# An autocorrelation layer in a pipeline of 16 pairs: the top-8 mask taken from the raw correlation, the bias copied into PSUM

## The reference, cut to what matters

```python
x = layernorm(x + attn(x))          # a 4-layer network of width 64, a scan over time, projection back to 512
x = layernorm(x + xattn(x, ctx))    # autocorrelation attention, below
x = layernorm(x + ffn(x))           # both factors quantised to MXFP4 in blocks of 32, product 512x512, + bias
```

```python
corr = ifft(fft(q) * conj(fft(k))).real          # over the 64 times, per channel
w, idx = top_k(corr, 8)                           # the 8 largest lags of each channel
w = softmax(w)
out = sum_i w[i] * v[min(idx[i] + t, 63)]         # values taken at shifted times
```

## Time and profile before

| what | value |
|---|---|
| median of three runs | 321.19 us |
| the profiled execution | 323.65 us |
| its span, first to last instruction | 321.6 us |
| mean granted TensorE clock | 0.978 |
| PE busy | 274.6 us (85%) |
| DVE busy | 269.8 us (84%) |
| ACT busy | 231.1 us (72%) |
| POOL busy | 174.7 us (54%) |

### The profile page before, as it was taken

The page is one execution under the profiler, slowest core; times in us unless marked ns, Lnnn a source line. Parts: engine busy times, 40 slices in busy tenths (PEclk is TensorE's granted clock), DMA queues, the critical chain, the costliest instruction groups (busy, mean ns, idle before and its releaser), DMA issues.

```text
span 321.6 us, 4437 instructions
## 1 busy us (share of the span) xinstructions
PE 274.6 (85%) x1060; PEld 109.8 (34%) x1060; DVE 269.8 (84%) x871; ACT 231.1 (72%) x541; POOL 174.7 (54%) x226
## 2 busy tenths in 40 slices
PE   1597988989889887888998999999998888977762
PEld 1223222322222222254433554434444244422220
DVE  5969989889888894358999999999999989869580
ACT  6046789899799797967666687778877776745534
POOL 1026513204204014023378888999999999997842
PEclk9999899999999999999999999999999999979987
DMA  6999999602113200600000000111101102011122
GB/s 207 396 273 354 325 160 213 128 23 65 36 33 85 78 0 17 116 1 2 2 0 16 17 14 6 50 49 18 51 34 51 51 16 51 34 50 49 51 82 99
DMA packets 22576, 26.54 MB, mean 83 GB/s; under 512 B 10771, under 2 KB 11411, under 8 KB 22550
## 3 DMA queue, kind: packets, MB, share of 16 engines
q1 hardware_dynamic: 20470, 22.06, 21.9%
q0 software_dynamic: 2080, 4.19, 7.7%
HBM read 15.89 MB, written 4.19 MB: 62 GB/s over the span
## 4 chain that ended last, share of the span: by engine, by line
DVE 30%; ACT 20%; PE 18%; issue 15%; POOL 11%; DMA 3%; SPq 1%; POOLq 0%; DVEq 0%; ACTq 0%
DVE big L1172 5%; DVE m L1153 4%; DVE X L1107 3%; DVE big L1142 3%; DMA big<-in_xT_dram 3%; PE ps L380 3%; ACT big L654 3%; DVE ps L1203 3%; ACT L752 2%; DVE ps L1081 2%; ACT X L682 2%; PE ps L562 2%; POOL big L925 2%; POOL big L931 2%; DVE big L1277 2%
## 5 line engine op out<-in xcount | busy, mean ns | idle before, releaser
L654 ACT ACTIVATE big<-X,lnv 128x512 f32<-128x512 f32 x48 | 34.2, 713 | 15.0 <-DVE X L1107 15.0
L1107 DVE SCALAR_TENSOR_TENSOR X<-ps,X 128x512 f32<-128x512 f32 x48 | 32.1, 682 | 10.7 <-PE ps L415 6.1
L391 PE MATMUL ps<-ctx_ring,consts 64*128 64x512 f32 (+1 forms) x96 | 35.8, 643 | 0.0
L441 PEld LDWEIGHTS ps<-consts,big 96*128 96x128 f32 x256 | 29.8, 191 | 13.4 <-issue 10.6
L441 PE MATMUL ps<-consts,big 96*128 96x64 f32 x256 | 32.0, 278 | 1.1 <-DVE big L1142 1.1
L1184 DVE TENSOR_TENSOR big<-ps,ctxf 128x512 f32<-128x512 f32 x48 | 30.8, 683 | 2.0 <-PE ps L475 1.3
L682 ACT ACTIVATE X<-X,lnv 128x512 f32<-128x512 f32 x32 | 25.8, 808 | 0.6
L1172 DVE MATCH_REPLACE8 big<-w,big 128x64 f32<-128x64 f32 x128 | 25.1, 210 | 0.0
L838 POOL TENSOR_TENSOR big<-big 128x512 f32<-128x512 f32 x4 | 5.8, 1444 | 35.5 <-DVE big L1250 25.5
L918 POOL TENSOR_TENSOR big<-big 128x512 f32<-128x512 f32 x15 | 19.0, 1268 | 6.2 <-DVE big L1172 6.0
L1142 DVE TENSOR_TENSOR big<-ps,ctxf 96x512 f32<-96x512 f32 x32 | 20.4, 677 | 0.8 <-PE ps L428 0.8
(11 more groups left out here) (188 smaller groups left out, 675.9 us busy)
## 6 DMA issues: line engine op xcount, KB each, us to landing
big<-in_xT_dram SPq DMA_DIRECT2D x4, 1024.0 KB, 9.4
ctx_ring<-in_ctx_dram SPq DMA_DIRECT2D x16, 256.0 KB, 4.0
out_dram<-X SPq DMA_DIRECT2D x16, 256.0 KB, 2.0
X<-in_x_dram SPq DMA_DIRECT2D x2, 1536.0 KB, 11.4
X<-rows_sb POOLq DMA_DIRECT2D x1, 3072.0 KB, 21.6
X<-in_wq_dram SPq DMA_DIRECT2D x1, 1024.0 KB, 5.6
X<-in_x_dram SPq DMA_DIRECT2D x2, 512.0 KB, 3.9
X<-rows_sb POOLq DMA_DIRECT2D x1, 1024.0 KB, 8.0
```

Of the source, the lines that this page charges most:

```text
L391: mm(bank(LANE_BANK[lane]), mat((CY_0, CY_1, CY_C)[f])[half, :], ctx_ring[half, r * N:(r + 1) * N], start=True, stop=True).then_inc(s_cfor ...
L441: last = mm(ps[:, 2 * N + j * P + b * L:2 * N + j * P + (b + 1) * L], PQ[0:EVEN, b * N + j * P:b * N + (j + 1) * P], mat(IC_E)[0:EVEN, 0:L ...
L654: squared[k, n] = chain(a(JUNK[k], row(n), ACT.Square, bias=st[:, 0:1], scale=-float(V), accum_out=st[:, 2:3]))
L1107: stt(row(m), bank(b), 0.0, row(m), ALU.add, ALU.add, accum_out=st[:, 0:1]).then_inc(s_sum[k], 1)
```

## The change

The network of the first 125 us is left as it is. In the pipeline:

- **The mask.** match_replace now runs on the raw correlation: `largest_taken` (once `without_largest`) replaces the eight maxima in `CR` by -3e38 (`TAKEN`) and writes `REST`. It needs the maxima only, not the exponentials. The masked weight is then `WN = (REST == TAKEN) * G`, one scalar_tensor_tensor on DVE for every pair (`chosen`). POOL's subtraction (L918), POOL's shifted maxima (L908) and ACT's exponential of them (L711) are gone, with `w8`. `CR` of a pair is now kept until its `REST` is written.
- **The rounding constant.** On DVE L1203 and L1204 become one tensor_tensor, `exponents`: `VB` and a one-element column `field` (broadcast), bitwise and, into `MB` in SBUF. The clip and multiply that was L1204 is a tensor_scalar on POOL in `clamped`.
- **The bias.** It was split into three bf16 rows and added by a matmul (L520). Now it is broadcast to 128 partitions by a second transfer into `rows_sb`, and ACT copies it in fp32 from SBUF into bank 1 (`bias_in`) after `fed` of the pair before; the four matmuls add onto it. The splitting on DVE in the first microseconds (L1056 to L1067) and one small transfer go.
- **The order of every loop.** The order of calls and their depths are new on PE, ACT, POOL and DVE. The counts of `kept_busy` change, and it now stands behind `feed_forward`.

```diff
-DRAIN_BUSY = ((0, 4), (6, 6), (5, 3))
+DRAIN_BUSY = {LAST + 7: 10, LAST + 8: 12}
+TAKEN = -3.0e38
+EXPONENT = 0x7F800000
@@ sync
-            sp.dma_start(rows_sb[0:SPLIT, V:2 * V], rows[V:2 * V].partition_broadcast(SPLIT)).then_inc(s_brow, 16)
-            sp.dma_start(rows_sb[:, 0:V], rows[0:V].partition_broadcast(P)).then_inc(s_rows, 16)
+            for k in range(2):
+                sp.dma_start(rows_sb[:, k * V:(k + 1) * V], rows[k * V:(k + 1) * V].partition_broadcast(P)
+                             ).then_inc(s_rows, 16)
...
-            for n in range(PAIRS + 3):
+            for n in range(PAIRS + 5):
                 quantized_to_channels(n)
-                stored(n - 3)
+                stored(n - 5)
@@ tensor, feed_forward
-                    if n >= 1:
-                        pe.wait_ge(s_sum[2], n)
-                    pe.wait_ge(s_magic[1], min(n + 2, LAST))
-                    mm(bank(1), ones[:, :], bias3[:, :], start=True, stop=False)
+                    pe.wait_ge(s_bias, n + 1)
@@ tensor, loop
-            for t in range(1, PAIRS + 11):
-                weights_to_time(t - 7)
-                out_even(t - 8)
-                weight_rest_forms(t - 7)
-                weight_forms(t - 7)
-                correlation(t - 5)
...
-                query_forms(t - 4)
-                feed_forward(t - 10)
...
-                quantized_to_channels(t - 9)
...
-                out_rest(t - 7)
-                projection(t)
+            for t in range(1, PAIRS + 10):
+                out_even(t - 6)
+                if t == 2:
+                    mixed(SLOTS)
+                    transposes(0, VC, bank(7), XQ[0])
+                weight_rest_forms(t - 5)
+                weight_forms(t - 5)
...
+                projection(t)
+                correlation(t - 3)
                 quantized_to_channels(t - 9)
+                feed_forward(t - 9)
+                query_forms(t - 2)
+                if t in DRAIN_BUSY:
+                    pe.wait_ge(s_sum[0], PAIRS)
+                    kept_busy(DRAIN_BUSY[t])
+                out_rest(t - 5)
+                weights_to_time(t - 4)
@@ scalar
+            def bias_in(n):
+                if here(n):
+                    if n == 0:
+                        act.wait_ge(s_rows, 32)
+                        act.wait_ge(s_hn, 2)
+                    else:
+                        act.wait_ge(s_sum[2], n)
+                    copy(bank(1), rows_sb[:, V:2 * V]).then_inc(s_bias, 1)
...
-                        act.wait_ge(s_m8, n - 1)
+                        act.wait_ge(s_mr, n - 1)
...
-                    a(w8[:, :], w8[:, :], ACT.Exp).then_inc(s_g, 1)
                     a(G, G, ACT.Exp).then_inc(s_g, 1)
...
-            for t in range(PAIRS + 10):
...
+            for t in range(-1, PAIRS + 9):
+                squares(1, t - 5)
+                factors(1, t - 5)
+                normalise(1, t - 5)
+                probabilities(t - 3)
+                corr_out(t - 2)
+                factors(0, t)
+                squares(2, t - 9)
+                last_factors(t - 9)
+                weights_out(t - 3)
+                top_exponentials(t - 2)
+                normalise(0, t)
...
+                log_sum(t - 2)
+                bias_in(t - 7)
+                squares(0, t + 1)
...
+                quantized_out(t - 8)
@@ gpsimd
-                    chain(g_.tensor_tensor(groups(w8[:, :], TOP), top, sh.broadcast_to([P, NG, TOP]), ALU.subtract))
...
-                    g_.tensor_tensor(WN, G, REST, ALU.subtract).then_inc(s_wn, 1)
...
+            def clamped(n):
+                if here(n) and n < LAST:
+                    pool.wait_ge(s_expo, n + 1)
+                    chain(g_.tensor_scalar(MB, MB, 0.25, MAGIC, ALU.max, ALU.mult))
+                    chain.then_wait(g_.tensor_scalar(VB, VB, 1.5, -1.5, ALU.min, ALU.max))
+                    halfway[n] = chain(g_.tensor_tensor(VB, VB, MB, ALU.add))
...
-            for t in range(PAIRS + 8):
-                block_scaled(t - 3)
-                chosen(t - 1)
-                top_differences(t)
-                finished(t - 7)
-                mark = clamped(t - 3)
-                differences(t)
-                rounded_off(t - 3, mark)
+            for t in range(PAIRS + 9):
+                differences(t - 1)
+                clamped(t - 4)
+                rounded_off(t - 4)
+                top_differences(t)
+                block_scaled(t - 3)
+                finished(t - 9)
@@ vector
+            def largest_taken(n):
+                if here(n):
+                    dve.wait_ge(s_m8, n + 1)
                     if n >= 1:
                         dve.wait_ge(s_wn, n)
+                    top = m8[:, n % 2 * NG * TOP:(n % 2 + 1) * NG * TOP]
                     for g in range(NG):
+                        last = v_.match_replace(REST[:, g * L:(g + 1) * L], top[:, g * TOP:(g + 1) * TOP],
+                                                CR[n % 2][:, g * L:(g + 1) * L], TAKEN)
                     last.then_inc(s_mr, 1)
...
-                    do(ts(bank(1).bitcast(I32), VB.bitcast(I32), 0x7F800000, None, ALU.bitwise_and))
-                    ts(MB, bank(1), 0.25, MAGIC, ALU.max, ALU.mult).then_inc(s_magic[1], 1)
+                    tt(MB.bitcast(I32), VB.bitcast(I32), field[:, 0:1].broadcast_to([P, V]), ALU.bitwise_and
+                       ).then_inc(s_expo, 1)
+            def chosen(n):
+                if here(n):
+                    dve.wait_ge(s_g, n + 1)
                     dve.wait_ge(s_mr, n + 1)
+                    if n >= 1:
+                        dve.wait_ge(s_wt, n)
+                    stt(WN, REST, TAKEN, G, ALU.is_equal, ALU.mult).then_inc(s_wn, 1)
...
-            for t in range(PAIRS + 9):
-                attended(t)
-                weight_products(t - 6)
-                block_scales(t - 7)
-                without_largest(t - 5)
-                last_chosen(t - 5)
-                fed(t - 9)
-                last_quantized(t - 7)
-                largest(t - 4)
-                if t == 6:
-                    last_norm(1, RS_LAST)
-                rounding(t - 7)
-                top_sum(t - 4)
-                query_products(t - 3)
-                crossed(t - 6)
+            for t in range(PAIRS + 10):
+                query_products(t - 3)
+                top_sum(t - 4)
+                crossed(t - 6)
+                exponents(t - 7)
+                last_quantized(t - 7)
+                largest_taken(t - 4)
+                weight_products(t - 5)
+                block_scales(t - 6)
+                attended(t)
+                if t == 5:
+                    last_norm(1, RS_LAST)
+                chosen(t - 4)
+                largest(t - 3)
+                fed(t - 9)
```

107 lines of the change are left out of this document (24 added, 83 removed).

## The result

The changed kernel takes 333.76 us in the median (330.56 to 337.26), the kernel before 321.24 beside it: ratio 1.0332, 95% interval 1.0218 to 1.0446. I had forecast 318.1 with a range up to 325. It is slower, and outside the range. One of its four runs, the 337.26, counts as a slow one, with a mean granted clock of 0.951 against 0.971 and more, and the ratio leaves it out; the median of the other three is 332.70.

The account below looks back on a forecast made before the run. VectorE's loop through ScalarE, no engine's load, was taken to set the 9.95 us period. First leg -6.2 and drain +3.1 gave -3.1 us: profiled 323.65 to 320.5, and 318.1 us against the median, 2.46 lower; range 311.5 to 325.

Parts of the forecast that it names:

- GpSimd's new instruction: GpSimd's clip and multiply in each pipeline period, priced at 0.61 us from the nearest row.
- It fits, barely: GpSimd's load in a period: 9.68 us becomes about 8.7, and 9.8 with both stops.
- The handoff in the drain: Pair 14 in the drain: transfer landed at 38.1 us, its feed-forward took 1.0, to 39.1.
- The holds: VectorE's two-SBUF-input instructions wait for GpSimd: `chosen` 0.14, `exponents` about 0.12 a period; eleven periods by 0.26, 2.9 us.
- the third rival: In the loop, `chosen` waits 1.05 us behind GpSimd's last instruction instead of 0.14: +9.1, 327.2 us; chance 0.18.
- its sign: Trace sign of the third rival in the loop: periods of over 10.2 us, with `chosen` at 1.5 and more.
- The ramp: Pipeline start: ScalarE finishes pair 0 before squaring pair 1, so the first query products start 0.9 us sooner.
- The loop through ScalarE: Between `crossed` and `block_scales`: 4.0 us of work now covers ScalarE's 2.7 us chain, so 3.7 us of waits go.
- ScalarE's copy: ScalarE's new 128x512 copy into PSUM, taken as 0.6 us, covered by idle time in the loop.
- The rest of the drain: GpSimd's rounding of pairs 12, 13, 14 is critical, ending at 35.6 us; last residual at 44.1 instead of 40.9.
- that rival: Drain at half the clock: twelve `kept_busy` cost 5.0 us, not 2.75: +2.3, 320.4 us; chance 0.20.
- Bias splitting and transfers: Transfers moved on SP's and GpSimd's queues: all put at nothing, well under 1 us if the cover were gone.

Follow-up runs that it names:

- experiment 1: Changed kernel with GpSimd's maximum and multiply in five forms by pair: minimum and maximum 0.61 us, maximum with multiply 1.93, a single operation 1.49.
- experiment 2: Changed kernel with GpSimd's maximum and multiply replaced by minimum and maximum, the multiply left out: 326.49 us, 1.0168 to the kernel before.
- 4: Changed kernel with the maximum and multiply moved back to VectorE, SBUF to SBUF: 334.97 us, 1.0344 to the kernel before.
- 7: Strided one-input `exponents`: first in the changed kernel with ScalarE multiplying and GpSimd clipping by minimum and maximum, 325.19 us; then alone in the changed kernel, 330.96 us.
- experiment 9: The first version of experiment 8 with `exponents` written to PSUM instead of SBUF: 322.19 us, 1.0006 to the kernel before.
- experiment 6: Kernel before, with only `crossed` put ahead of the query products in VectorE's order: 328.66 us, 1.0242.
- experiment 8: New drain order and 4 fillers instead of 22: first version, on the first kernel of 7, 320.88 us; second, on the changed kernel, 331.06 us.
- experiment 10: `largest` put ahead of `chosen` on VectorE: first version, on experiment 9's kernel, 322.60 us; second, on the first version of experiment 8, 323.98 us.

## Why the prediction was wrong

Against the forecast for the profiled execution, 320.5, it came out at 330.56. Of these 10.1 us the last query products carry 3.3 (272.02 against 268.7) and the drain 6.7 (50.8 against 44.1). Some 1.3 us of the second belong to the loop: GpSimd's period stays at 10.75, but when the last `attended` has gone and `chosen` is down from 1.51 to 0.77, VectorE's query products move forward in it, once, by a period of 9.40. Two steps failed, the price of one instruction and a handoff put at nothing.

- **GpSimd's new instruction: the first step that failed.** The prediction took 0.61 from the "nearest row". That row was the same instruction kind, shape and type, but another pair of operations, and the trace shows 1.92 for this one (experiment 1: 1.93). "It fits, barely" then became a GpSimd without idle time, and no rival had GpSimd's own load as the bound. The unknown cost should have had two ends; the row of 1.27 for a sum was no upper end either. At the price of 0.61 (experiment 2) 4.0 of the 10.1 us go, and the time is still 326.49, above the range: this step alone does not explain the miss.
- **The handoff in the drain: the second.** The forecast let the feed-forward of pair 14 start when its transfer landed, at 38.1. `fed(13)` stands behind `last_quantized`, and the bias copy that the feed-forward needs stands behind `fed(13)`; the sum has no term for it. In experiment 2, where the instruction costs what I had taken, the last query products come 0.4 from the forecast (partly luck: nine periods of 10.05 instead of 9.86, after a ramp 1.3 better) and the drain is 50.1 instead of 44.1. Of these 6.0 us, 2.1 are GpSimd's rounding (37.7 instead of 35.6), 3.0 this handoff and 1.0 what follows it. In the changed kernel the rounding is so late (42.1) that the handoff adds only 0.6 to it.
- **The holds: too small.** I forecast 0.26 a period for VectorE from one phase worked out. In the long periods of the changed kernel VectorE loses 0.8 on `chosen` alone (in the periods before them nothing), and in those of experiments 2, 4, 7 and 9 it loses 0.6 to 0.8, whichever instruction is repaired. The mechanism was named rightly, and the third rival, `chosen` behind GpSimd's last instruction with a point of decision at 0.3 us, is what experiment 9 shows line by line. It was given 0.18. In the changed kernel itself its sign came (periods over 10.2, `chosen` at 1.5), but `chosen` met the sum L918 there and not the last instruction, as GpSimd was 1.3 later than I had it.
- **The ramp: right.** The seventh query products came at 179.27; 268.7 less nine periods of 9.86 puts them at 180.0. From there nine periods took 92.75 us, 10.31 each instead of 9.86.
- **The loop through ScalarE: right.** L1081's wait is gone. The change of order did need TensorE's new order with it, as experiment 6 shows.
- **ScalarE's copy: right,** 0.58 in the loop, 0.60 in the drain, where I took 0.6.
- **The rest of the drain.** I had the rounding of pairs 12 to 14 on GpSimd as the critical thing. It ends at 314.13, 42.1 after the last query products, where I had 35.6: 3.9 are three times 1.3 for the slow form, the other 2.6 I put down to holds, to the 1.3 that belong to the loop and to what queued behind them, without a run that tells them apart. From there to the last residual it took 8.7 (forecast 8.5), which looks right and is so by chance, since the last stretch ran by another chain. The twelve fillers cost 2.75 as said, at full clock, so that rival fell.
- **Bias splitting and transfers: nothing shown.** The first residual of the pipeline came 1.4 us sooner than before (124.70 against 126.06), but in the other runs it lies anywhere from 124.7 to 126.6 with the change and from 125.0 to 125.9 without the new bias, so this is no effect of it.

What stays open: the spread of the changed kernel's runs, what one form of GpSimd's instruction does that another does not, and how the 3.7 us of experiment 8 divide among the parts of its edit.

## What to carry to other kernels

The price of a GpSimd tensor_scalar went by its operations here: take it from a row with the same operations, or give it two ends; a minimum-maximum pair cost a third of a maximum-multiply pair, and the multiply could move to ScalarE. Where VectorE and GpSimd both run near the period, moving an instruction that reads and writes SBUF can cost more than its duration: in experiments 2, 4, 7 and 9 most of the loss went to the next one that met GpSimd, whatever form the first got, and sending the operand through PSUM only moved it. It ended when `chosen` and GpSimd's instruction were set apart in time. Find the meeting in order of time, and move it in the steady state only: in the ramp the same swap cost 1.2 us, and in one trace clock as well. And when one delay in a drain is mended, look at once for the one right behind it: two that run side by side hide each other.

## What the hardware showed that I had not expected

- GpSimd, 128x512 fp32 in SBUF: minimum and maximum 0.614 us, maximum and multiply or multiply and maximum 1.93, maximum alone or multiply alone 1.49 (experiment 1). Two operations can be faster than one.
- VectorE writing PSUM from one SBUF input was never held (0.68 to 0.70, experiment 9). The same operation into SBUF was held by 0.27 in the late stretch of experiment 8, first version, and `finished` beside it took 1.19 instead of the 0.76 of experiment 9; set apart in time (experiment 10, second version), they took 0.62 and 0.77.
- After the same two waits of TensorE, 1.6 and 0.7 us, the clock fell to its lower level in one profiled execution and stayed full in another (experiment 10).
- Making GpSimd faster did not shorten the period by itself: in experiment 9 it waits 1.65 us in each and still meets `chosen`.
